# Query projections by seven products of half size instead of eight, with five of their inputs streamed from DRAM

## The reference, cut to what matters

```python
h_q = (x @ w_q.T).reshape(b, lq, H, DH)
h_k = (key_value_states @ w_k.T).reshape(b, lk, H, DH)
h_v = (key_value_states @ w_v.T).reshape(b, lk, H, DH)
score = jnp.einsum('bqhd,bkhd->bhqk', h_q, h_k) + position_bias[None]
score = softmax(where(mask, score, -inf))
attn = jnp.einsum('bhqk,bkhd->bqhd', score, h_v).reshape(b, lq, H * DH)
out = attn @ w_out.T
```

## Time and profile before

| | us |
|---|---|
| median of 3 runs | 829.47 (828.86 to 829.69) |
| the profiled execution | 830.24 |
| its span | 828.1 |
| PE busy | 820.7 |
| POOL busy | 536.9 |
| DVE busy | 449.4 |
| ACT busy | 446.7 |

### The profile page before, as it was taken

One profiled execution on the slowest core, in us unless ns is written; L12 is line 12 of the kernel. 1 busy time (PEld: TensorE's weight loads), 2 busy tenths in 40 slices (PEclk: granted clock), 3 DMA queues, 4 the chain that ended last, 5 costly groups with the idle time before them and its releaser, 6 DMA issues.

```text
span 828.1 us, 15838 instructions
## 1 busy us (share of the span) xinstructions
PE 820.7 (99%) x4730; PEld 721.5 (87%) x4730; DVE 449.4 (54%) x761; ACT 446.7 (54%) x1301; POOL 536.9 (65%) x556
## 2 busy tenths in 40 slices
PE   8999999999999999999999999999999999999998
PEld 7888888988899888988889888998889888898887
DVE  6976544355634656245553555346562455626683
ACT  6856564464726555364644647356553546437632
POOL 1587777467875768756685578757687567865440
PEclk9999999999999999999999999999999999999999
DMA  9403322122211323123231222113230232311102
GB/s 312 136 17 101 112 80 67 55 92 67 94 36 59 98 68 97 25 70 97 75 96 54 90 68 92 38 54 97 69 97 25 70 97 68 107 42 46 47 18 89
DMA packets 50917, 64.59 MB, mean 78 GB/s; under 512 B 10864, under 2 KB 36848, under 8 KB 49872
## 3 DMA queue, kind: packets, MB, share of 16 engines
q1 hardware_dynamic: 50608, 63.81, 25.0%
q10 hardware_dynamic: 288, 0.52, 0.2%
HBM read 44.37 MB, written 4.19 MB: 59 GB/s over the span
## 4 chain that ended last, share of the span: by engine, by line
PE 89%; ACT 4%; SPq 3%; DMA 2%; DVE 2%; issue 1%; ACTq 0%; DVEq 0%
PE w_ps L1235 41%; PE o_ps L1235 35%; PE s_ps L1271 6%; PE s_ps L1277 6%; SPq L352 2%; ACT p_blocks L671 2%; ACT p_blocks L622 1%; DMA wo_raw<-ctx_dram 1%; DMA pT<-p_blocks 1%; PE w_ps L1292 0%; ACT kT L622 0%; PE s_ps L1235 0%; PE w_ps L1334 0%; DVE stats L935 0%; DVE p L1026 0%
## 5 line engine op out<-in xcount | busy, mean ns | idle before, releaser
L550 POOL TENSOR_SCALAR picked<-codes 128x256 f32<-128x256 int32 x112 | 126.3, 1128 | 19.2 <-POOL level L553 15.6
L515 POOL TENSOR_TENSOR p<-pos_raw,mask_add 128x1024 f32<-128x1024 f32 x32 | 69.9, 2185 | 104.5 <-ACT p_blocks L671 104.0
L671 ACT ACTIVATE p_blocks<-p,neg_max 128x128 f32<-128x128 f32 x248 | 96.1, 389 | 51.6 <-DVE neg_max L1028 43.0
L553 POOL TENSOR_TENSOR level<-level,picked 128x256 f32<-128x256 f32 x112 | 88.7, 792 | 20.8 <-POOL picked L550 20.8
L487 POOL TENSOR_TENSOR ring_lo<-k_raw,ring_hi 128x256 fp32r<-128x256 f32 x105 | 76.5, 741 | 27.4 <-ACT ring_hi L622 24.5
L622 ACT ACTIVATE ring_hi<-k_raw 128x256 fp32r<-128x256 f32 x105 | 38.7, 412 | 103.0 <-POOL k_raw L477 103.0
L1051 DVE TENSOR_TENSOR resid<-o_ps,resid 128x512 f32<-128x512 f32 x102 | 68.6, 685 | 43.3 <-PE o_ps L1235 43.1
L1235 PE MATMUL w_ps<-ctx_hi,ring_hi 128*128 128x512 f32 x210 | 84.7, 403 | 0.5 <-ACT kT L622 0.5
L1235 PE MATMUL w_ps<-ctx_hi,ring_lo 128*128 128x512 f32 x210 | 82.0, 391 | 0.0
L1235 PE MATMUL w_ps<-ctx_lo,ring_hi 128*128 128x512 f32 x210 | 81.7, 389 | 0.0
L622 ACT ACTIVATE p_blocks<-p_blocks,row_scale 128x128 f32<-128x128 f32 x248 | 77.0, 390 | 0.0
(11 more groups left out here) (235 smaller groups left out, 2295.2 us busy)
## 6 DMA issues: line engine op xcount, KB each, us to landing
pT<-p_blocks SPq DMA_DIRECT2D x480, 32.0 KB, 1.8
wv_raw<-wv_dram SPq DMA_DIRECT2D x8, 1024.0 KB, 4.8
q_raw<-q_dram SPq DMA_DIRECT2D x32, 256.0 KB, 3.3
wo_raw<-wo_dram SPq DMA_DIRECT2D x32, 256.0 KB, 3.9
k_raw<-k_dram SPq DMA_DIRECT2D x15, 512.0 KB, 3.5
resid<-x_dram SPq DMA_DIRECT2D x2, 1024.0 KB, 10.9
pos_raw<-pos_dram SPq DMA_DIRECT2D x32, 64.0 KB, 3.8
out_dram<-resid SPq DMA_DIRECT2D x7, 256.0 KB, 2.0
```

The costliest lines, as they stand in the source:

```text
L515: pool.tensor_tensor(p[:, :, :], pos, mask_add[:, :, :], ALU.add).then_inc(bias_done, 1)
L550: then(pool.tensor_scalar((level if code == 0 else picked)[:, :], codes[:, :], float(code), NF4[code], match, ALU.mult))
L553: then(pool.tensor_tensor(level[:, :], level[:, :], picked[:, :], ALU.add))
L671: e = act.activation(out(b), p[:, b, :].rearrange("p (k c) -> p k c", c=Q), ACT.Exp, bias=neg_max[:, b:b + 1], accum_out=prob_sum[:, b:b + 1])
```

## The change

- From pair 3 on (heads 5 to 31), the queries of a pair are made by seven products too (q0 to q6, `query_product`): 42 matmuls of 512 columns. Pairs 0 to 2 stay plain.
- The seven inputs don't fit in SBUF. `xn` has four places of 1 MB (high and low part): two hold blocks that stay (for q0 and q5), and places X and Y are refilled from DRAM five times a pair, by transfers that POOL issues (`stream_x`, `stream_y`): X with S1 (q1), S3 (q3), D (q6), Y with S2 (q2), S4 (q4). Each is issued once PE is past the product that used the place (`queries_past`), and PE waits for its landing.
- In the first round, DVE makes the four sums in eight halves (`input_sum`, 20 instructions of 512 columns), ACT and POOL split them (`sum_high`, `sum_low`) and SP stores them to DRAM (`store_sum`).
- The query weights' splits are ACT's (`split_qp`) and DVE's, their sums DVE's (`query_sum`), ACT copies (`copy_queries`) and DVE adds the products (`add_queries`), as for keys.
- The lists of all engines are reordered around this. On PE, k6 and q6 come in the even head; the attend is in two parts around q6. On POOL the decode parts of odd heads are spread between the streams, and in even heads decode comes last. `wo_raw` has one place instead of two. The output tiles of the loop use other banks.
- The probabilities go through DRAM: two stores of 128 partitions and four loads for each head (`move`), in place of 16 transfers. ACT's `exps` wait for the stores only.

```diff
 PRODUCTS = 7
+FIRST = 3
+PLACE_X, PLACE_Y = 2, 3
+INPUT_AT = (0, PLACE_X, PLACE_Y, PLACE_X, PLACE_Y, 1, PLACE_X)
+QUERY_ORDER = (1, 0, 2, 3, 4, 5, 6)
+QUERIES_AT = tuple(QUERY_ORDER.index(p_at) + 1 for p_at in range(PRODUCTS))
+X_BLOCKS, Y_BLOCKS = 3, 2
+STREAM_AT = {1: 1, 3: 2, 6: 3, 2: 1, 4: 2}
+DRAM_S1, DRAM_S2, DRAM_S3, DRAM_S4, DRAM_D = range(5)
+SUM_HALVES = ((DRAM_S1, 0), (DRAM_S2, 0), (DRAM_S4, 0), (DRAM_S3, 0), (DRAM_S1, 1), (DRAM_S2, 1), (DRAM_S4, 1), (DRAM_S3, 1))
...
-        xn_lo = sb("xn_lo", [P, C, T], f32r)
...
+        xn = sb("xn", [P, 4, 2, 2, HT], f32r)
...
-            def move_blocks(keys):
-                for k in keys:
-                    for i in range(NQ):
-                        sp.dma_start(pT[Q * k:Q * (k + 1), i, :, :],
-                                     p_blocks[Q * i:Q * (i + 1), k, :, :]).then_inc(pT_loaded, 16)
+            def move(h):
+                for pair in range(2):
+                    sp.wait_ge(p_turned_done, 2 * h + pair + 1)
+                    if pair == 0:
+                        sp.sem_inc(sp_passed, 1)
+                        sp.wait_ge(pT_loaded, LOADS * h)
+                    sp.dma_start(blocks_d[pair], p_blocks[:, 2 * pair:2 * pair + 2, :, :]).then_inc(blocks_stored[pair], STORE)
+                sp.wait_ge(attn_done, 2 * h)
+                sp.sem_inc(sp_passed, 1)
+                for pair in range(2):
+                    sp.wait_ge(blocks_stored[pair], STORE * (h + 1))
+                    for k in range(2):
+                        at = 2 * pair + k
+                        sp.dma_start(pT[Q * at:Q * (at + 1), :, :, :],
+                                     blocks_d[pair, :, k, :, :].rearrange("(i r) b c -> r i b c", i=NQ)).then_inc(pT_loaded, 16)
...
+            def stream(place, block_at, streamed):
+                pool.dma_start(xn[:, place, :, :, :], input_d[block_at]).then_inc(streamed, 16)
...
+            def queries_past(m, p_at):
+                passed(qp_done, PRODUCTS * m + QUERIES_AT[p_at])
...
+            def odd_head(g, j, last):
+                h = G * g + j
+                m = 2 * g + (j + 1) // 2
+                at = (g, 2) if j == 1 else (g + 1, 0)
+                queries_past(m, 1)
+                stream_x(DRAM_S3)
+                decode(*at, slice(0, 1))
+                queries_past(m, 2)
+                stream_y(DRAM_S4)
+                next_bias(h, j, g)
+                decode(*at, slice(1, 2))
+                split_k(m, 4, key_slot(j, 4))
+                decode(*at, slice(2, 3))
+                queries_past(m, 3)
+                stream_x(DRAM_D)
+                split_k(m, 5, key_slot(j, 5))
+                split_k(m, 6, key_slot(j, 6))
+                if not last:
+                    queries_past(m, 4)
+                    stream_y(DRAM_S2)
+                decode(*at, slice(3, 4))
+            def even_head(g, j, last):
+                h = G * g + j
+                m = 2 * g + j // 2
+                if j == G:
+                    next_values(g + 1)
+                if not last:
+                    queries_past(m, 6)
+                    stream_x(DRAM_S1)
+                next_bias(h, j, g)
+                if j == 2:
+                    if not last:
                         start_of_pair(m + 1, 3)
                         go_on_pair(m + 1, 3)
+                    decode(g, 3)
+                else:
+                    go_on_values(g + 1, lambda: None)
+                    decode(g + 1, 1)
...
+                act.wait_ge(qp_done, PRODUCTS * m + {4: QUERIES_AT[1], 5: QUERIES_AT[0], 6: QUERIES_AT[4]}.get(p_at, 0))
+                copy(query_weights(p_at)[0], q_raw[:, WEIGHT_AT[p_at], :]).then_inc(qp_hi_done, 1)
...
+                    for pair in range(2):
+                        act.wait_ge(blocks_stored[pair], STORE * h)
...
+                m = 2 * g + (j + 1) // 2
+                if j == 1:
+                    act.wait_ge(values_done, 2 * PRODUCTS * (g + 1))
+                else:
+                    act.wait_ge(out_done, B * (2 * g + 1))
+                split_qp(m, 2)
+                split_qp(m, 3)
+                split_wo(0, h - 1)
+                exps(h, 0, by_blocks)
+                copy_queries(m, 0)
+                copy_queries(m, 1)
+                split_qp(m, 4)
+                exps(h, 1, by_blocks)
+                normalise(h, 0, by_blocks)
+                copy_keys(m, 0)
+                copy_queries(m, 2)
+                normalise(h, 1, by_blocks)
+                attention(2 * (h - 1), j - 1, 0, s_flat(0))
+                copy_keys(m, 1)
+                copy_keys(m, 2)
+                attention(2 * (h - 1) + 1, j - 1, 1, s_flat(1))
+                split_k(m, 4, key_slot(j, 4))
+                split_k(m, 5, key_slot(j, 5))
+                split_qp(m, 5)
+                split_k(m, 6, key_slot(j, 6))
...
+                for hf in range(2):
+                    normalise(h, hf, by_blocks)
+                act.wait_ge(qp_added, ADDS * (m + 1))
+                copy_keys(m, 3)
+                if last:
+                    return
+                for p_at in range(2):
+                    split_qp(m + 1, p_at)
+                if j == 2:
+                    for p_at in range(4):
+                        split_k(m + 1, p_at, key_slot(3, p_at))
+                    return
...
+            def add_queries(m, n):
+                out, copied, bank, p_at, copies = ((qT[:, half(1)], qT[:, half(1)], 0, 3, 1),
+                                                   (qT[:, half(0)], qT[:, half(0)], 1, 4, 3),
+                                                   (qT[:, half(0)], first_product, 2, 5, 2))[n]
+                dve.wait_ge(qp_done, PRODUCTS * m + QUERIES_AT[p_at])
+                dve.wait_ge(qp_copied, COPIES * m + copies)
+                if n == 2:
+                    dve.wait_ge(scores_done, 2 * (2 * m) + 2)
+                dve.tensor_tensor(out, o_ps[bank][:, :], copied, ALU.add).then_inc(qp_added, 1)
...
+                    add_pair(o, b, loop_tiles)
+                    if b == 1:
+                        turn_blocks(h)
+                    if b == 3:
+                        split_qp(m + 1, 0)
+                        query_sum(0, m + 1)
+                    if b == 4:
+                        query_sum(1, m + 1)
+                    if b == 5:
+                        split_qp(m + 1, 1)
+                        query_sum(2, m + 1)
...
+            def query_product(m, p_at):
+                pe.wait_ge(qp_lo_done, PRODUCTS * m + p_at + 1)
+                if p_at in STREAM_AT:
+                    streamed, blocks = (x_streamed, X_BLOCKS) if INPUT_AT[p_at] == PLACE_X else (y_streamed, Y_BLOCKS)
+                    pe.wait_ge(streamed, 16 * (blocks * (m - FIRST) + STREAM_AT[p_at]))
+                hi, low = query_weights(p_at)
...
+                pairs = [((hi[:, s * DH:(s + 1) * DH], low[:, s * DH:(s + 1) * DH]),
+                          (xn[:, at, 0, s, :], xn[:, at, 1, s, :])) for s in range(2)]
+                three(o_ps[BANK_OF[p_at]][:, :], pairs, OPENS[p_at]).then_inc(qp_done, 1)
...
+                pe.wait_ge(keys_copied, COPIES * m)
+                pe.wait_ge(qp_added, ADDS * m)
+                pe.wait_ge(qp_copied, COPIES * m)
+                pe.wait_ge(attn_lo_done, 2 * (h - 1) + 2)
+                scores(h, 0)
+                if j == 1:
+                    pe.wait_ge(values_added, 2 * ADDS * (g + 1))
+                else:
+                    pe.wait_ge(out_added, B * (2 * g + 1))
+                query_product(m, 1)
+                if j == 1:
+                    pe.wait_ge(values_copied, 2 * COPIES * (g + 1))
+                query_product(m, 0)
+                key_product(m, 0, key_slot(j, 0))
+                pe.wait_ge(qp_copied, COPIES * m + 2)
+                query_product(m, 2)
+                key_product(m, 1, key_slot(j, 1))
+                pe.wait_ge(pT_loaded, LOADS * h)
+                for hf in range(2):
+                    pe.wait_ge(biased, 2 * h + hf + 1)
+                    attend(j - 1, hf, s_flat(hf), moved)
+                pe.wait_ge(keys_copied, COPIES * m + 1)
+                key_product(m, 2, key_slot(j, 2))
+                pe.wait_ge(qp_copied, COPIES * m + 3)
+                query_product(m, 3)
+                pe.wait_ge(keys_copied, COPIES * m + 3)
+                key_product(m, 3, key_slot(j, 3))
+                query_product(m, 4)
+                key_product(m, 4, key_slot(j, 4))
+                query_product(m, 5)
...
+                pe.wait_ge(keys_added, ADDS * m + 2)
+                pe.wait_ge(qp_added, ADDS * m + 2)
+                pe.wait_ge(attn_lo_done, 2 * (h - 1) + 2)
+                scores(h, 1)
+                key_product(m, 6, key_slot(j - 1, 6))
+                pe.wait_ge(pT_loaded, LOADS * h)
+                for hf in range(2):
+                    pe.wait_ge(biased, 2 * h + hf + 1)
+                    attend(j - 1, hf, s_flat(hf), moved)
+                    if hf == 0:
```

(20 more changed lines are left out.)

697 lines of the change are left out of this document (486 added, 211 removed).

## The result

| | kernel before | changed kernel |
|---|---|---|
| median of 4 runs, us | 829.51 (828.86 to 829.69) | 993.07 (991.36 to 994.85) |
| profiled execution's span, us | 828.1 | 989.6 |
| PE busy, us | 820.7 | 862.3 |
| mean granted clock | 1.00 | 0.924 |

The ratio is 1.1968, with a 95% interval of [1.1954, 1.1982]. The direction was right; the size was not, and the time lies above the range of 845 to 930.

The account below looks back on a forecast made before the run. The prediction took PE's issue order to bound the loop. Its terms, 830.24 + 37 (six rounds) + 2.5 (first round) + 4.7 (tail) + 7 (clock) = 881.4 us, gave a median of 881, range 845 to 930.

Parts of the forecast that it names:

- PE saves 2.6 a round: PE in the loop: six fewer query matmuls a pair, less one late start, 1.3 us a pair, 2.6 a round.
- The refill takes 5.8 us from the issue: POOL's 1 MB transfers: 1.0 us of POOL's time to issue plus 4.8 to landing; bounds 4.8 and 10.9.
- The rival of slow refills: Refills in the loop: each takes 10.9 us, 16.6 a round longer, some 960 us in all; chance 0.10.
- POOL is free at 12.4 of head j = 3, q3 waits 6.4: Head j = 3: decode part 3 ends 12.4 us after its scores, q3's refill lands at 18.2, PE waits 6.4.
- POOL is free at 7.6 of head j = 1, q3 waits 1.6: Head j = 1: decode part 1 behind the values ends at 7.6 us, q3's refill lands at 13.4, PE waits 1.6.
- The refill for q4: Place Y in odd heads: no wait of PE at q4 was forecast.
- The check by POOL's sum of work: POOL in a round: 87 us of work plus 14 of waits, more than a round of 94.6 can hold.
- ACT and DVE at no cost: Loop: ACT's added 3.3 us a round and DVE's 10 fit under PE; nearest chain q2, waiting for ACT's copy.
- The clock, +7: PE's clock falling after the 6.4 us waits: between 0 and 2.4 us for six waits, the middle, +7 us.
- The first round, +2.5: First round: added sums and splits delay k3 and a softmax, 3.6 us less old waits, +2.5 (0 to 8).
- The tail, +4.7: Scores of head 29 to those of head 31: 32.8 us against 28.1, +4.7, with ACT's last key copy late.
- The probabilities' way at nothing: Probabilities' two stores and four loads a head in place of 16 moves: no effect on the loop's time.

Follow-up runs that it names:

- experiment 12: experiment 10 with its refills and PE's waits for them left out, so queries come from wrong input blocks: 827.9 us, ratio 0.9975.
- experiment 10: Changed kernel, decode parts back ahead, part 3 partly earlier still, ACT's key weight 0 split earlier, first-round sums later, first two refills mid-values: 833.7 us.
- experiment 2: Changed kernel with the refill for q4 issued right behind q3's, ahead of the decode's first step: 967.4 us, ratio 1.1663.
- experiments 2 and 7: 7: changed kernel with the five refills of a round issued by ACT, POOL's order unchanged: 923.7 us, ratio 1.1134.
- experiment 3: Changed kernel with decode part 3 back ahead of the keys and part 1 ahead of the values on POOL: 869.0 us, ratio 1.0487.
- experiment 6: Changed kernel with useless matmuls on PE ahead of q3 and q4 of the odd heads, to keep PE busy: 979.7 us, ratio 1.1811.
- experiment 8: Kernel before with only the probabilities' way through DRAM put in, in place of sixteen moves within SBUF: 827.93 us, ratio 0.998.
- experiments 10 and 11: 11: experiment 10's spread decode, with first-round sums, stores and first refills placed once more and the last key copy ahead of the scalings: 834.3 us.
- experiment 1: Changed kernel without the refills and PE's waits for them, so queries come from wrong input blocks: 910.7 us, ratio 1.098.

## Why the prediction was wrong, step by step

- **PE saves 2.6 a round: right.** With nothing in its way the loop takes 94.60 us (experiment 12) against 97.28: 2.7.
- **The refill takes 5.8 us from the issue: right in the median, wrong where it matters once a round.** 5.4 measured (5.0 to 9.8), of which POOL is held 0.61; but the one for q4 in head j = 1 took 9.3 to 9.8 in heads 9 to 25. The Trainium skill's fit ("DMA: Bandwidth & Descriptors", section on the SWDGE path) made it 4.4. The rival of slow refills (10.9 each, 0.10) did not come true as a whole. The interference between GpSimd and a VectorE instruction with two SBUF inputs that the Trainium skill ("SBUF — State Buffer", section Who interferes with whom) tells of shows here, and is small. POOL's addition below takes 0.74 us where DVE runs nothing with two inputs in SBUF, and DVE's sum 0.42; side by side, in the changed kernel, both are longer:

```profile
459.45 0.97 POOL L626 TENSOR_TENSOR ring_lo<-k_raw,ring_hi 128x256 fp32r<-128x256 f32 x1
```

```profile
459.93 0.77 DVE L1287 TENSOR_TENSOR q_raw<-q_raw 128x256 f32<-128x256 f32 x1
```

Over 218 to 610 us this comes to little: the same low halves of POOL took 741 ns on average before and 755 in experiment 10, where DVE is busy 260 us of 400 instead of 204.
- **POOL is free at 12.4 of head j = 3, q3 waits 6.4: right in its mechanism.** 13.4 and 7.6.
- **POOL is free at 7.6 of head j = 1, q3 waits 1.6: right too.** 8.2 and 2.85.
- **The refill for q4: this is the step that failed.** The prediction gave q4 no wait at all, and it waits 4.3 us in head j = 3 and 3.0 in head j = 1. The list for head j = 3 ended at q3. What POOL does between the two refills, the first step of a decode, was taken only as 2.2 us of work in head j = 1, never as a wait. But it depends on SP's loads, they depend on decode part 3's end, and part 3 was the very thing that had moved. The prediction followed the moved instructions forward on POOL and did not follow what their end releases on another queue. In head j = 1 it was the landing that was mis-sized, 9.4 us instead of 5.8 behind another refill. Of the 17.2 us a round that were missed (24.5 against 6.1 and 1.2 for the clock) these two waits are 7.3, the lower clock behind all four waits 8.1 more than taken, and the waits for q3 2.5; 0.7 taken for k5 did not come. By experiments 2 and 7 q4's wait can't be counted apart, as other victims (key weight 4) stand behind it; the whole delay of POOL's order, the clock included, is 20.8 us a round (experiment 3), where 8.7 and 1.2 for the clock were predicted. Experiment 2 shows that q4's wait in head j = 3 comes from standing behind the decode's step. No run loads the codes sooner with the order kept, so what the wait for them costs by itself is not measured.
- **The check by POOL's sum of work** (87 + 14 against 94.6) pointed the right way with the wrong reason: POOL does that work in 95.6 (experiment 10), since the waits moved when the order did.
- **ACT and DVE at no cost: right in the changed kernel,** and not in the mended order, where ACT's copy for q2 was the next wait (3.5 us a round in experiment 3). The prediction had named that chain as the nearest.
- **The clock, +7: too small.** In the trace it is 9.3 us a round; what mending it gives back is 13 us of 164 (experiment 6). It fell after all four waits in four of the six rounds and after three of them in the other two, where one was forecast: the mean clock was 1.00 in 666.20 to 669.17 us, behind a wait of 2.94, and in 795.90 to 803 us, behind one of 2.13.
- **The first round, +2.5: 6.5.** The waits for ACT and DVE in it are 7.1 us, where 3.6 were taken. Behind it, in head 5, the first refill, issued at the end of POOL's values, made q1 wait 3.55 us, with the clock at 0.51 for the 5.35 us after that (171.25 to 176.60); the text had no term for it.
- **The tail, +4.7: 10.3,** by the prediction's own cut, from the scores of head 29 to those of head 31 (931.46 - 893.09 = 38.4 against 28.1; 32.8 predicted). Head 30 took 10.5 where 10.6 was predicted, with the 4.0 us wait for kT where it was foretold. Head 29 took 27.8 where 22.2 was predicted: it waits 2.3 us for q3 and 2.0 for q4 and works at the lower clock behind them.
- **The probabilities' way at nothing:** 1.8 us faster (experiment 8).

The sum, in the profiled executions: 6.5 + 143.7 + 11.3 = 161.5 for a predicted 2.5 + 37 + 7 + 4.7 = 51.2. Nine tenths of the miss, 100 us of 110, are in the rounds.

What stays open: how the first round's loss, 14.3 us with head 5, divides. Two other placements of its sums won 2.6 us of it at most (experiments 10 and 11), and no version moved the sums out of the round.

## What to carry to other kernels

When work is moved back on an engine, follow its end as well as its place: which queue it releases, what that queue loads, and who waits for the load in front of whom. A refill is as late as the last thing ahead of its issue, and later again if another large transfer is under way (9.4 us instead of 5.4). A wait removed from one product goes to the next in the queue until the order itself is mended; so test the order first (two moved calls, 124 us) and the transfers after (82 us in a bad order, 6 in a good one). And a clock that falls in waits is worth mending by filling only where the engine that idles sets the pace; here POOL's order did.

## What the runs showed of the hardware

- PE had four waits a round, of 2.1 to 8.2 us, and behind all but two of the 24 it worked in part at 1.2 GHz. In one round the granted clock was 0.69 and 0.64 in the two stretches behind those of head j = 3, and 0.72 and 0.76 behind those of j = 1 (545 to 551 and 551 to 558 us). With filling in their place the mean over the whole rose from 0.924 to 0.988.
- A 1 MB refill from DRAM held POOL 0.61 us at the issue and landed after 5.4 us (median of 65; 6.0 in experiment 10, whose loop moves 207 GB/s), but after 9.3 to 9.8 where it was issued 3.4 us behind another and some 9.9 right behind one (experiment 2); issued by ACT it held ACT 0.33 us and landed after 4.9.
- In the changed kernel, from 200 to 700 us, POOL's additions of 256 columns in decode took 0.75 us at most where DVE ran no sum or difference of two inputs in SBUF beside them, and up to 1.22 where it did.
- A 64 KB load of absmax took 4.9 us to landing in the changed kernel, where it runs beside a refill issued within 2 us of it, and 2.5 to 2.8 in the kernel before, in experiment 1 (no refills) and in experiment 3 (refills elsewhere). So of the 7.5 us from decode's end to its next first step (468.93 to 476.46) some 2.4 are this company, and the rest is the store, the issues and a plain landing; without refills the same wait is still 5.25.
